# A scale of K for every batch, and x statistics, context maxima, Newton steps and loads spread over the phases, in a fused cross-attention and expert kernel

## The reference

```python
q = Wq @ layernorm(x) + bq;  k = Wk @ ctx + bk;  v = Wv @ ctx + bv   # per batch, 16 heads of 16
q, k = rope(q), rope(k)
prob = softmax(q^T k / 4)                                            # per head, 512 x 512
x = x + tanh(g_xattn) * (Wm @ (prob v) + bm)
h = layernorm(x)                                                     # 2048 tokens of 512
top2 of h @ gate_w -> weights cw                                     # 8 experts
out = x + tanh(g_ffn) * sum_e cw[e] * ((silu(h @ w0[e]) * (h @ w1[e])) @ wo[e])
```

## Time and profile before

| | |
|---|---|
| median of 3 runs | 1223.23 us (1220.42 to 1226.88) |
| profiled execution, its own time | 1225.35 us |
| its span | 1223.5 us |
| PE busy | 1109.7 us, 91% |
| DVE busy | 801.3 us, 65% |
| ACT busy | 683.8 us, 56% |
| POOL busy | 370.8 us, 30% |
| mean granted clock of PE | 0.938 of full speed |
| chain that ended last | PE 76%, ACT 10%, DVE 6%, issue 4%, DMA 2% |

### The profile page before, as it was taken

The page is one execution under the profiler, slowest core; times in us unless marked ns, Lnnn a source line. Parts: engine busy times, 40 slices in busy tenths (PEclk is TensorE's granted clock), DMA queues, the critical chain, the costliest instruction groups (busy, mean ns, idle before and its releaser), DMA issues.

```text
span 1223.5 us, 17328 instructions
## 1 busy us (share of the span) xinstructions
PE 1109.7 (91%) x5417; PEld 443.2 (36%) x5417; DVE 801.3 (65%) x1559; ACT 683.8 (56%) x932; POOL 370.8 (30%) x443
## 2 busy tenths in 40 slices
PE   3796898999999999988728999999999999999996
PEld 1221333333333333322223444444444444444442
DVE  7786787878786877887465365665646665564631
ACT  2165677777776777777505265655536564462521
POOL 4544464757473837312310111111111111101001
PEclk8678999999998999998658999999999999999999
DMA  5544334212131313132346566676747676564333
GB/s 197 159 164 134 132 133 158 88 62 98 54 104 64 102 44 132 53 106 87 104 182 161 109 171 174 155 191 148 192 74 203 139 202 141 134 195 78 67 57 59
DMA packets 189942, 153.16 MB, mean 125 GB/s; under 512 B 130336, under 2 KB 150944, under 8 KB 189856
## 3 DMA queue, kind: packets, MB, share of 16 engines
q1 hardware_dynamic: 178656, 130.36, 36.7%
q0 software_dynamic: 7744, 18.09, 7.9%
q10 hardware_dynamic: 3456, 3.64, 0.9%
HBM read 73.34 MB, written 41.75 MB: 94 GB/s over the span
## 4 chain that ended last, share of the span: by engine, by line
PE 76%; ACT 10%; DVE 6%; issue 4%; DMA 2%; POOL 0%; SPq 0%; ACTq 0%; DVEq 0%; POOLq 0%
PE psum L1168 31%; PE psum L1178 15%; PE psum L337 7%; ACT wh L476 7%; PE psum L324 6%; PE psum L221 5%; PE psum L312 3%; PE psum L264 3%; DVE MX L659 2%; PE psum L231 2%; PE psum L282 2%; ACT wh L433 1%; PE psum L246 1%; ACT Xr L469 1%; DVE bst L633 1%
## 5 line engine op out<-in xcount | busy, mean ns | idle before, releaser
L1168 PE MATMUL psum<-wh,xT 128*128 128x512 f16 x1728 | 383.0, 382 | 16.5 <-DVE xT L1250 16.5
L659 DVE TENSOR_REDUCE MX<-psum 128x2 f32<-128x1024 f32 x256 | 310.2, 1220 | 97.7 <-PE psum L312 96.6
L476 ACT ACTIVATE wh<-psum,es 128x512 f32<-128x512 f32 x512 | 320.7, 687 | 94.0 <-PE psum L324 88.8
L1168 PEld LDWEIGHTS psum<-wh,xT 128*128 128x128 f16 x1728 | 170.0, 98 | 223.5 <-issue 22.6
L1178 PE MATMUL psum<-wh,hT 128*128 128x512 f16 x864 | 194.0, 381 | 3.5 <-DMA hT<-hn 3.5
L324 PE MATMUL psum<-stg 50*128 50x512 f16 x512 | 152.2, 407 | 35.8 <-ACT wh L476 21.8
L1332 POOL DMA_INDIRECT out<-yb,target x36 | 56.2, 1561 | 339.1 <-ACT yb L1209 331.5
L1282 DVE TENSOR_TENSOR hh<-sg,psum 128x512 f32<-128x512 f32 x72 | 49.3, 685 | 158.6 <-ACT sg L1199 158.6
L337 PE MATMUL psum<-wh,vT 128*32 128x512 f32 x1024 | 147.2, 649 | 0.0
L539 ACT ACTIVATE wh<-stg,scw 128x1024 f16<-128x1024 f32 x96 | 103.0, 1138 | 48.9 <-DVE c L591 33.5
L546 DVE SCALAR_TENSOR_TENSOR wh<-stg,scw,wh 128x1024 f16<-128x1024 f32 x96 | 118.6, 1291 | 17.6 <-ACT wh L539 17.6
(11 more groups left out here) (197 smaller groups left out, 1023.1 us busy)
## 6 DMA issues: line engine op xcount, KB each, us to landing
stg<-in_w SPq DMA_DIRECT2D x16, 2048.0 KB, 10.2
stg<-in_wo SPq DMA_DIRECT2D x8, 2048.0 KB, 10.6
stg<-scr SPq DMA_DIRECT2D x186, 64.0 KB, 2.3
Xs<-zero SPq DMA_DIRECT2D x40, 264.0 KB, 2.8
wh<-wh SPq DMA_DIRECT2D x64, 128.0 KB, 2.0
scr<-wh SPq DMA_DIRECT2D x32, 256.0 KB, 2.4
xs<-in_x SPq DMA_DIRECT2D x8, 512.0 KB, 5.7
out<-xs SPq DMA_DIRECT2D x8, 512.0 KB, 3.1
```

Of the source, the lines that this page charges most:

```text
L476: act.activation(m.Pb[:, c % 2, hh, :], m.psT[tile % 2], ACT.Exp, scale=m.es[:, min(hb // 2, 2):min(hb // 2, 2) + 1]).then_inc(S["exped"], 1)
L659: dve.tensor_reduce(m.MX[:, hb % 2, c0:c0 + 9:8], m.psS[tile % 2], AX_X, ALU.max, negate=True).then_inc(S["maxed"], 1)
L1168: last = pe.matmul(m.psum[:, 2 * j + w, :], m.xT[:, 4 * xp + k, :], m.wh[(e % 2, w)][:, wp, c:c + 512], start=(k == 0 and xp == 0 and wp = ...
```

## The change

Every batch gets a scale of K of its own, so the context maximum of batch b is needed for b alone. Its parts are spread out: DVE's maximum over the context of batch b goes to step 1 of phase 2b - 4; SP's write to HBM and read back to the same phase; the maximum over 128 numbers and the scale to step 4 of phase 2b - 3; the two row statistics of x to steps 3 and 5 of phase 2b - 5, the aggregation and first guess to its step 12; the Newton steps to the head of POOL's phase 2b - 4. x of batch b is loaded by SP at the end of phase 2b - 7, the context of batch b at the end of phase 2b - 6. In what was phase 0 of SP's queue, the swap of k for block 3 now stands ahead of the stack of block 2, and eight fills follow each other.

```diff
-        n = 1 + min(hb // 2, 2) if w else 0
+        n = 1 + hb // 2 if w else 0
...
-    for b in range(2, 5):
-        load_ctx(act, m, S, io, b)
+    load_ctx(act, m, S, io, 2)
...
-    def guesses():
+    def guess(b):
 
         step.settle()
-        for i in range(6, 16):
+        if b > 3:
+            dve.wait_ge(S["rstd_far"], b - 3)
+        for i in range(2 * b, 2 * b + 2):
             step.more(dve.bn_aggr(m.mv[:, i, :], m.bst[:, i, :]))
         step.settle()
-        step(dve.tensor_scalar(m.vx[:, :], m.mv[:, 6:16, 1], EPS, None, ALU.add))
+        step(dve.tensor_scalar(m.vx[:, :], m.mv[:, 2 * b:2 * b + 2, 1], EPS, None, ALU.add))
         step(dve.tensor_scalar(m.yxi[:, :], m.vx[:, :].bitcast(I32), 1, None, ALU.arith_shift_right))
-        dve.tensor_scalar(m.rstd[:, 6:16].bitcast(I32), m.yxi[:, :], -1.0, float(0x5F3759DF), ALU.mult, ALU.add).then_inc(S["x_guess"], 1)
+        dve.tensor_scalar(m.rstd[:, 2 * b:2 * b + 2].bitcast(I32), m.yxi[:, :], -1.0, float(0x5F3759DF), ALU.mult, ALU.add).then_inc(S["x_guess"], 1)
...
     def spread(ph, s):
-        if ph == 0 and s < NB - 2:
-            step.more(ctx_rows(m.rest[:, s:s + 1], s + 2))
-        if ph == 0 and s == NB - 2:
-            step.settle()
-            dve.tensor_reduce(m.big[:, 8:9], m.rest[:, :], AX_X, ALU.max).then_inc(S["far_rows_largest"], 1)
-        if ph == 1 and s == 6:
-            dve.wait_ge(S["far_read"], 16)
-            dve.tensor_reduce(m.bigs[:, 8:9], m.farb[:, :], AX_X, ALU.max).then_inc(S["far_largest"], 1)
-            dve.wait_ge(S["far_largest"], 1)
-            k_scale(2)
-        if ph == 1 and s < 10:
-            stats(6 + s, 7 + s)
-        if ph == 1 and s == 12:
-            guesses()
+        b = (ph + 4) // 2
+        if ph % 2 == 0 and 2 <= b < NB and s == 1:
+            ctx_rows(m.big[:, 6 + b:7 + b], b).then_inc(S["ctx_rows_largest"], 1)
+        b = (ph + 3) // 2
+        if ph % 2 and 2 <= b < NB and s == 4:
+            dve.wait_ge(S["far_read"], 16 * (b - 1))
+            dve.tensor_reduce(m.bigs[:, 6 + b:7 + b], m.farb[:, :], AX_X, ALU.max).then_inc(S["far_largest"], 1)
+            dve.wait_ge(S["far_largest"], b - 1)
+            k_scale(b)
+        b = (ph + 5) // 2
+        if ph % 2 and 3 <= b < NB and s in (3, 5):
+            stats(2 * b + s // 5, 2 * b + s // 5 + 1)
+        if ph % 2 and 3 <= b < NB and s == 12:
+            guess(b)
...
-    def far_roots():
-        pool.wait_ge(S["x_guess"], 1)
-        newton(pool, step, m.rstd[:, 6:16], m.yxa[:, :], m.vx[:, :]).then_inc(S["rstd_far"], 1)
-        pool.wait_ge(S["rstd_far"], 1)
+    def far_root(b):
+        pool.wait_ge(S["x_guess"], b - 2)
+        newton(pool, step, m.rstd[:, 2 * b:2 * b + 2], m.yxa[:, :], m.vx[:, :]).then_inc(S["rstd_far"], 1)
+        pool.wait_ge(S["rstd_far"], b - 2)
...
-        if ph == 2:
-            far_roots()
         b = (ph + 4) // 2
         if ph % 2 == 0 and 2 <= b < NB:
-            pool.wait_ge(S["rstd_near"], 1)
+            if b == 2:
+                pool.wait_ge(S["rstd_near"], 1)
+            else:
+                far_root(b)
...
+    def far_write(b):
+
+        sp.wait_ge(S["ctx_rows_largest"], b)
+        if b > 2:
+            sp.wait_ge(S["far_read"], 16 * (b - 2))
+        sp.dma_start(m.far.rearrange("(p n) -> p n", n=1), m.big[:, 6 + b:7 + b]).then_inc(S["far_written"], 16)
+
+    def far_read(b):
+        sp.wait_ge(S["far_written"], 16 * (b - 1))
+        if b > 2:
+            sp.wait_ge(S["far_largest"], b - 2)
+        sp.dma_start(m.farb[:, :], m.far.rearrange("(p n) -> p n", p=1).to_broadcast([128, 128])).then_inc(S["far_read"], 16)
...
-    for b in range(5, NB):
-        load_ctx(sp, m, S, io, b)
...
     keep(1, 2)
+    far_write(2)
+    swap(1, 3)
     stack(sp, m, S, 0, 2)
     stack(sp, m, S, 1, 2)
-    for b in range(3, NB):
-        load_x(sp, m, S, io, b)
-    sp.wait_ge(S["far_rows_largest"], 1)
-    sp.dma_start(m.far.rearrange("(p n) -> p n", n=1), m.big[:, 8:9]).then_inc(S["far_written"], 16)
-    sp.wait_ge(S["far_written"], 16)
-    sp.dma_start(m.farb[:, :], m.far.rearrange("(p n) -> p n", p=1).to_broadcast([128, 128])).then_inc(S["far_read"], 16)
-    for ph in range(0, LAST + 1):
-        a = ph + 3
-        if 0 < ph and ph + 2 < NH:
+    far_read(2)
+    keep(0, 3)
+    max_rows(2)
+    load_x(sp, m, S, io, 3)
+    keep(1, 3)
+    fill_rows(0)
+    fill_rows(4)
+    load_ctx(sp, m, S, io, 3)
+    for ph in range(1, LAST + 1):
+        a, b = ph + 3, (ph + 4) // 2
+        if ph + 2 < NH:
             stack(sp, m, S, 0, ph + 2)
             stack(sp, m, S, 1, ph + 2)
...
-        if 0 < ph and a < NH:
+        if a < NH:
             swap(0, a)
-        if 0 < ph < NH:
+        if ph < NH:
...
+        if ph % 2 == 0 and b < NB:
+            far_write(b)
...
+        if ph % 2 == 0 and b < NB:
+            far_read(b)
...
+        if ph % 2 and ph <= 7:
+            load_x(sp, m, S, io, (ph + 7) // 2)
+        if ph % 2 == 0 and ph <= 8:
+            load_ctx(sp, m, S, io, (ph + 6) // 2)
```

More of the change, by code:

```diff
@@ L148, in attention @@
         self.ve, self.y, self.yi, self.ya = sb("ve", [128, 2]), sb("y2", [128, 2]), sb("yi", [128, 2], I32), sb("ya", [128, 2])
-        self.vx, self.yxi, self.yxa = sb("vx", [128, 10]), sb("yxi", [128, 10], I32), sb("yxa", [128, 10])
+        self.vx, self.yxi, self.yxa = sb("vx", [128, 2]), sb("yxi", [128, 2], I32), sb("yxa", [128, 2])
         self.L, self.IX, self.IF = sb("L", [128, 2, 8]), sb("IX", [128, 2, 8], U32), sb("IF", [128, 2, 2])
@@ L155, in attention @@
         self.bq, self.bv, self.bm, self.gx = sb("bq", [128, 2, 2]), sb("bv", [128, 2]), sb("bm", [128, 2]), sb("gx", [128, 1])
-        self.big, self.bigs, self.rest = sb("big", [128, 9]), sb("bigs", [128, 9]), sb("rest", [128, NB - 2])
+        self.big, self.bigs = sb("big", [128, 6 + NB]), sb("bigs", [128, 6 + NB])
         self.farb = sb("farb", [128, 128])
         self.F, self.byx, self.byb = sb("F", [128, 1]), sb("byx", [128, 2]), sb("byb", [128, 2])
-        self.bound, self.p2, self.sc = sb("bound", [128, 4]), sb("p2", [128, 4]), sb("sc", [128, 4])
-        self.sbias, self.es, self.es0 = sb("sbias", [128, 4, 2]), sb("es", [128, 3]), sb("es0", [128, 1])
+        self.bound, self.p2, self.sc = sb("bound", [128, 1 + NB]), sb("p2", [128, 1 + NB]), sb("sc", [128, 1 + NB])
+        self.sbias, self.es, self.es0 = sb("sbias", [128, 1 + NB, 2]), sb("es", [128, NB]), sb("es0", [128, 1])
         self.wmT = sb("wmT", [128, 2, 256])
@@ L475, in exps @@
             act.wait_ge(S["weighed"], group - 1)
-        act.activation(m.Pb[:, c % 2, hh, :], m.psT[tile % 2], ACT.Exp, scale=m.es[:, min(hb // 2, 2):min(hb // 2, 2) + 1]).then_inc(S["exped"], 1)
+        act.activation(m.Pb[:, c % 2, hh, :], m.psT[tile % 2], ACT.Exp, scale=m.es[:, hb // 2:hb // 2 + 1]).then_inc(S["exped"], 1)
     def sums(i):
@@ L865, in ctx_rows, with k_scale @@
         return dve.tensor_reduce(to, m.cx[b].rearrange("p t n -> p (t n)"), AX_X, ALU.max, apply_absolute_value=True)
-    def k_scale(n):
-        if n == 1:
+    def k_scale(b):
+        if b == 1:
             dve.wait_ge(S["ctx_largest"], 1)
-        scale(1 + n, m.bigs[:, 6 + n:7 + n]).then_inc(S["k_scale"], 1)
+        scale(1 + b, m.bigs[:, 6 + b:7 + b]).then_inc(S["k_scale"], 1)
     dve.memset(m.epst[:, :], EPS).then_inc(S["eps"], 1)
```

## The result

The changed kernel took 1209.55 us (median of 9, 1200.92 to 1216.22) beside 1223.23 us for the kernel before (median of 9): a ratio of 0.988, 95% interval 0.985 to 0.992. The forecast was 1213.4, in a range of 1207 to 1222. A later set of 4 runs of the same changed kernel gave 1211.50 (ratio 0.9915, 0.9886 to 0.9944). So the gain is 11 to 14 us, where 9.8 were forecast. Its profiled execution took 1207.78 us around a span of 1205.9, against 1225.35 and 1223.5: 17.6 us of span less, more than the medians show.

What follows compares the result with a forecast made beforehand. PE bounds settled phases; the losses were an 8.11 us gap from SP's queue, the low clock behind it and a long phase 1. Eight items summed to -9.8 us: 1225.35 to 1215.5, or 1213.4 on the median's scale; range 1207 to 1222.

Steps and rivals of the forecast that it cites:

- Item 1: End of phase 0: score maxima no longer wait behind SP's x loads and far read, closing PE's gap; gain 8.1 us.
- Item 2: Phase 1: shorter without the low clock and with two statistics in place of ten; gain 6.9 us (4.9 to 8.9).
- Item 3: Step 8 of phase 1: score maxima arrive late behind SP's fills, stacks and swap; cost 0.6 us (0 to 3).
- the second rival: Phase 1: the stall moves to the second half's score maxima, with a low clock again; 1220.6 us, chance 0.20.
- Item 4: Phase 0: VectorE loses five of its six context maxima; gain 0.5 us (0 to 6.0).
- Item 5: Phases 2, 4, 6, 8, 10, step 1: context maxima ahead of copy mT delay L246; cost 4.0 us (0 to 6.0).
- Item 6: Odd phases 3 to 9: VectorE's added scales, statistics and start values mostly hidden in its idle time; cost 0.8 us.
- losing the cover: Odd phases: VectorE becomes the bound and its added work costs 5.5 us each; 1238 us, chance 0.08.
- Item 7: Phases 4, 6, 8, 10: twelve Newton operations ahead of POOL's normalisation; cost 0.3 us (0 to 2).
- Item 8: SP's extra load, write and read issues, 0.5 us each, lie where SP waits anyway; no cost.

Runs made afterwards that it cites:

- e1: Kernel before, with SP's far read and the x loads of batches 3 to 7 behind the score maxima in phase 0; 1210.6 us, ratio 0.990.
- e4: Changed kernel plus five context maxima of batch 2, results unread, in steps 0 and 2 to 5 of phase 0; 1207.33 us, ratio 0.9883.
- e6: Changed kernel plus a second dozen of GpSimd Newton instructions on scratch in phases 4, 6, 8 and 10; 1214.96 us, ratio 0.9915.
- e10: Changed kernel plus ten unread statistics of batch 2's x in steps 0 to 9 of phase 1, no transfer moved; 1214.39 us, ratio 0.9905.
- e3: Changed kernel with the ten x statistics back in phase 1 and their x loads back early in phase 0; 1217.07 us, ratio 0.9947.
- e7: Changed kernel plus two statistics and nine small VectorE instructions, all unread, in each of phases 3, 5, 7 and 9; 1262.39 us, ratio 1.0317.
- e12: Changed kernel plus nine small unread VectorE instructions at steps 4 and 12 of phases 3, 5, 7 and 9; 1251.30 us, ratio 1.0228.
- e13: Changed kernel plus nine small unread VectorE instructions, all at step 8 of phases 3, 5, 7 and 9; 1214.28 us, ratio 0.9932.

## Why the prediction was right, step by step

- **Item 1, the gap, -8.1: right**, and shown alone in e1. The score maxima went out at 81.69, five us sooner than I had reckoned (86.9). e1 moves the read and the loads at once, and which of the two held the queue how long is not shown.
- **Item 2, phase 1, -6.9 (4.9 to 8.9): right within its range.** L221 to L221 it fell by 4.6 in the first profile and by 5.5 in the second, and item 3's wait is inside the 4.6; for the two items together I had 6.3. In e4 and e6 it fell by 2.0 and 1.9 only, with the low clock in it. But the two causes are not the two I added. The statistics account for 5.7 (e10 against the second profile), for 5.2 at least. Starting at full clock gave nothing in e1, where DVE still had its ten statistics: the clock fell at the wait at step 8 instead.
- **Item 3, step 8, +0.6 (0 to 3): right in place and kind,** 1.00 us in the first profile and none in the second, where PE came later. It was the most fragile spot: 4.93 us in e3. What I had left to the second rival, a low clock behind this wait, is what e4 and e6 show behind 0.70 and 1.32 us; phase 1 took 3.5 us more there than in the second profile.
- **Item 4, phase 0's maxima, -0.5: right for its own reason, short on the phase.** Five maxima put back cost 1.0 us at the same clock (e4 against two profiles). Phase 0 is shorter by 2.4 us beyond the gap, on average over ten profiles, since in five of them the low clock that covered 67 to 77 us comes shorter or not at all. Whether the gapless programs get this more often is open: e1 has it with the old DVE work and the x loads moved, but one profile of the kernel before is too few to say what it usually gets.
- **Item 5, context maxima ahead of the copy, +4.0: the step that failed.** L246 did move, by 0.5 in phases 2 and 6, and I charged that to the phase's end. In its place the runs show zero. The pair of L324 behind L246 in phase 2, before and then after:

```profile
144.02 0.91 PE L324 MATMUL psum<-stg 50*128 50x512 f16 x2
```
```profile
125.29 0.39 PE L324 MATMUL psum<-stg 50*128 50x512 f16 x2
```

  It ends 6.05 us into the phase before and 6.07 after. The pair used to have half a microsecond of pause inside it, and starts half a microsecond later now. I had seen that PE waits for ScalarE there, but took the wait to lie before the flipped scores of 277.52 and let it cover 0.2 of the 1.2; it lay inside the pair right behind L246.
- **Item 6, odd phases, +0.8: low, but no further off than a profile can tell,** +1.6 in the first profile. The second's sum is 174.5, or +2.6, but an odd phase that no edit touched moves by over 2 us between profiles: phase 5 took 33.4 us in e4 and e6 and 35.8 in the second profile, and e4's five sum to 167.4. The price of losing the cover was far too low: I said 5.5 a phase, and e7 paid 10 to 14.
- **Item 7, GpSimd, +0.3: right,** even phases within 0.2. Its reserve is smaller than the 3.2 us that I read from the queue: 3.3 us more cost 0.9 a phase (e6).
- **Item 8: right.** No row shows a cost.

Two us ahead of phase 0 stood in no item. In the first profile the projection in phase -1 ran partly at full clock. Over all profiles phase 0 starts between 57.8 and 60.2, so this is not the change's.

So -9.8 came from -14.9 in phases 0 and 1, where the nine profiles that share these phases have -15.5 on average, and +5.1 behind them, in the even and odd phases, where the two profiles of the changed kernel have +1.4 and +2.4. The mechanism was right, and item 5 was mis-sized: 4.0 for what measured zero.

One thing stays open. By its median the gap-only kernel is as fast as the whole change (ratios 0.990 and 0.988 to 0.9915), though the change's two profiles save 4 to 5 us more in phase 1. With phase 0 taken in, e1 needs 68.2 us where the nine profiles have 61.6 to 64.7. Odd phases take 1.4 to 2.5 of these back. And e1's profile needs 752.7 us from phase 12 on, which no edit touches, where the changed kernel's two need 755.5 and 755.3; over all profiles this part took 752.3 to 755.8. The rest is below what these runs can tell.

## What to carry to other kernels

A delay of an instruction is a cost only if it survives the next wait of the same engine: follow it to the next place where that engine already stood for someone else, and subtract that wait whole. Price a transfer in an in-order queue by everything that stands behind it; moving one wait and five loads here was worth nearly the whole change. And place an engine's small instructions by what GpSimd is doing beside them: nine of them cost 1 us a phase in one place and 9 in another.

## What the runs showed of the hardware

- A DVE tensor_scalar on 128x2 takes 0.17 to 0.26 us alone. Issued while GpSimd works on 128x512 or 128x1024, it lasts until GpSimd's current instruction ends: 1.04 us on average beside the rotary work, and 1.97 for L655 in e12, which ends at 196.19 as GpSimd's instruction does at 196.17. The same operation on 128x1 was not held: in e13's phase 3, L851 to L855 took 0.15 to 0.27 us each while GpSimd worked, and L858 on 128x2, right behind them, 1.12. The Trainium skill says that whichever of a tensor_scalar in a two-port mode and a GpSimd instruction issues first holds the shared ports for its whole length and blocks the other (SBUF — State Buffer, Who interferes with whom). The trace agrees for 128x2 behind a GpSimd instruction that has begun, with the times above. What I had not expected is what it does to a phase: in e12, 7.9 us of small instructions stretched phase 3 by 13.2 us, since PE waited 3.50 and 6.01 us for DVE at two places, and ran at a granted clock of 0.50 (1.2 GHz) from 170 to 182 and again from 194 to 202.
- The granted clock is not the program's alone. Two executions of one program differed in it from 64 to 74 us, and by 3.5 us in the phase; their even phases 2 to 10, at full clock, agreed within 0.1 us.
